# Moving the query tokens' reciprocal norms through DRAM instead of two selection matmuls, in a gated linear-attention block

## What is computed

```
q, k, v = conv4(silu(x @ Wq)), conv4(silu(x @ Wk)), conv4(silu(x @ Wv));  z = x @ Wz;  a = x @ Wa;  b = x @ Wb
q, k = rope(q), rope(k)
q = q / max(norm(q), 1e-12);  k = k / max(norm(k), 1e-12)        # per token and head
for s in range(4):                                                # four lags
    attn = sum_d(q[t] * k[t - s]) / sqrt(128)
    out[t] += attn * sigmoid(a[t - s] * b[t]) * v[t - s]
out = out * rms(out) * norm_w * silu(z);   result = out @ Wout
```

## Time and profile before

| | us |
|---|---|
| median of 3 runs | 1431.97 |
| the profiled execution's own time | 1433.0 |
| span of its trace | 1431.2 |
| PE busy in the span | 1398.2 (98%) |
| DVE, ACT, POOL busy | 1027.4, 733.4, 404.0 |
| steps of the attention stage | from about 48 to about 1005, 14.55 a step in the middle |

### The profile page before, as it was taken

One profiled execution on the slowest core, in us unless ns is written; L12 is line 12 of the kernel. 1 busy time (PEld: TensorE's weight loads), 2 busy tenths in 40 slices (PEclk: granted clock), 3 DMA queues, 4 the chain that ended last, 5 costly groups with the idle time before them and its releaser, 6 DMA issues. The chain is left out here.

```text
span 1431.2 us, 23209 instructions
## 1 busy us (share of the span) xinstructions
PE 1398.2 (98%) x7048; PEld 1166.4 (82%) x7048; DVE 1027.4 (72%) x1597; ACT 733.4 (51%) x2146; POOL 404.0 (28%) x504
## 2 busy tenths in 40 slices
PE   6999999999999999999999999997999999999998
PEld 4778888888888888888888888886788888788886
DVE  7889999999999999999989999995122222234442
ACT  5655655556655556565565665553554444332221
POOL 6152443434434344434443443422000000000001
PEclk9999999999999999999999999998899999999999
DMA  9123334433344233433334333333331101065454
GB/s 298 38 73 83 95 75 103 96 80 94 74 103 95 73 95 73 110 88 81 88 82 109 88 79 90 80 75 82 128 115 52 44 22 44 22 184 166 144 166 157
DMA packets 103962, 137.60 MB, mean 96 GB/s; under 512 B 11248, under 2 KB 48112, under 8 KB 103664
## 3 DMA queue, kind: packets, MB, share of 16 engines
q1 hardware_dynamic: 94704, 120.28, 29.4%
q0 software_dynamic: 9216, 16.78, 6.7%
HBM read 61.53 MB, written 25.17 MB: 61 GB/s over the span
## 5 line engine op out<-in xcount | busy, mean ns | idle before, releaser
L428 POOL TENSOR_TENSOR rnorm<-norms,neg_half 128x8 f32<-128x8 f32 x64 | 126.8, 1982 | 353.1 <-DVE norms L660 353.1
L635 DVE SCALAR_TENSOR_TENSOR y_k<-u_k,cw_k,y_k 128x512 f32<-128x512 f32 x192 | 159.6, 831 | 26.4 <-ACT y_k L533 18.1
L635 DVE SCALAR_TENSOR_TENSOR y_v<-u_v,cw_v,y_v 128x512 f32<-128x512 f32 x192 | 172.7, 899 | 6.9
L553 ACT ACTIVATE bank<-bank 128x128 f32<-128x128 f32 x512 | 133.6, 261 | 85.7 <-PE bank L826 85.7
L1137 DVE TENSOR_TENSOR hid_lo<-relu,hid_hi 128x512 fp32r<-128x512 f32 x64 | 44.3, 692 | 179.0 <-ACT hid_hi L1083 179.0
L635 DVE SCALAR_TENSOR_TENSOR y_q<-u_q,cw_q,y_q 128x512 f32<-128x512 f32 x192 | 144.4, 752 | 31.6 <-ACT y_q L533 23.5
L1055 POOL TENSOR_TENSOR g_buf<-g_buf,up_raw 128x512 f32<-128x512 f32 x3 | 3.8, 1282 | 411.0 <-DVE g_buf L1158 411.0
L1178 DVE TENSOR_TENSOR hid_lo<-o_raw,hid_hi 128x512 fp32r<-128x512 f32 x64 | 44.3, 692 | 102.9 <-ACT hid_hi L1103 102.9
L1079 ACT ACTIVATE relu<-bank,us_sb 128x512 f32<-128x512 f32 x64 | 44.0, 688 | 127.9 <-PE bank L1218 127.9
L1103 ACT ACTIVATE hid_hi<-o_raw 128x512 fp32r<-128x512 f32 x64 | 40.4, 632 | 123.5 <-PE bank L1248 120.8
L1233 PE MATMUL bank<-down_sign,hid_hi 128*128 128x512 f32 x256 | 101.4, 396 | 0.3 <-DVE hid_lo L1137 0.3
(11 more groups left out here) (173 smaller groups left out, 3565.5 us busy)
## 6 DMA issues: line engine op xcount, KB each, us to landing
swapped_q<-y_q SPq DMA_DIRECT2D x128, 128.0 KB, 2.3
swapped_k<-y_k SPq DMA_DIRECT2D x128, 128.0 KB, 2.3
sq_sum<-out_sq POOLq DMA_DIRECT2D x64, 256.0 KB, 3.4
o_scratch<-o_buf SPq DMA_DIRECT2D x64, 256.0 KB, 2.5
o_raw<-o_scratch SPq DMA_DIRECT2D x64, 256.0 KB, 3.2
raw_q<-in_wq SPq DMA_DIRECT2D x16, 256.0 KB, 3.1
raw_k<-in_wk SPq DMA_DIRECT2D x16, 256.0 KB, 3.6
raw_v<-in_wv SPq DMA_DIRECT2D x16, 256.0 KB, 4.5
```

The costliest lines, as they stand in the source:

```text
L428: nc.gpsimd.tensor_tensor(rnorm[:, g1 % 2, :], norms[:, g1 % 2, :], neg_half[:, 0:2 * BC], ALU.pow).then_inc(root_done, 1)
L553: last = nc.scalar.activation(block_of, block_of, ACT.Square, accum_out=norms[:, g1 % 2, i * BC + b:i * BC + b + 1])
L635: nc.vector.scalar_tensor_tensor(y[n][:, g % 2, :], u[n][:, g % 2, i:i + CH], cw[n][:, bass.ds(h * TAPS + i, 1)], y[n][:, g % 2, :], ALU.m ...
```

## The change

The reciprocal norms of the query tokens take another way. Once POOL has them (`root_done`), SP stores those of the group to a small DRAM scratch, `rq_scratch[g]`, as rows of 4 numbers (the four blocks of the group) per token, 128 rows, with four more rows behind them that hold the first four tokens of the following block. That is three DMAs: the group's own 128 x 4, the 4 x 3 of the blocks within it, and the 4 x 1 that the group before lacked (zeros behind the last group). A step later in the pipeline one load brings each partition 8 rows (128 B): the 4 from the multiple of four at or below its token, and the next 4. Those rows overlap, four partitions read the same ones. POOL masks the 8 rows with a constant table (`window`: from the own token on in the first four, before it in the second), adds the two halves, and multiplies by gate_k. The result is `gates`, which DVE uses as before. Gone are rq_x, rq_parts, sel_r, both matmuls, the copy that made sel_r, and DVE's join and product. The floor of the norms moves from DVE to POOL, and POOL's wait for gate_done to its first gate_k.

```
 # SP, step(h, g), ahead of the swaps
+                if at := back(h, g, 1):
+                    g1 = at[1]
+                    wait(sp, root_done, c)
+                    own = rnorm[:, g1 % 2, 0:BC]
+                    sp.dma_start(rq_scratch[g1, 0:P, :], own).then_inc(rq_stored, 16)
+                    sp.dma_start(rq_scratch[g1, P:P + LAGS, 0:BC - 1], own[0:LAGS, 1:BC]).then_inc(rq_stored, 16)
+                    first = own[0:LAGS, 0:1] if g1 > 0 else rot["q"][0:LAGS, S:S + 1]
+                    sp.dma_start(rq_scratch[(g1 - 1) % G, P:P + LAGS, BC - 1:BC], first,
+                                 allow_slow_non_contiguous=True).then_inc(rq_stored, 16)
 # SP, behind the swaps, ahead of the output's store
+                if at := back(h, g, 2):
+                    g2 = at[1]
+                    wait(sp, rq_stored, 48 * (c if back(h, g, 1) else c - 1))
+                    runs = bass.AP(tensor=rq_scratch.tensor, offset=rq_scratch[g2].offset,
+                                   ap=[[LAGS * BC, P // LAGS], [0, LAGS], [1, WIN * BC]])
+                    sp.dma_start(rq_win[:, g2 % 2, :, :].rearrange("p j b -> p (j b)"), runs).then_inc(rq_in, 16)
 # POOL, step(h, g)
                 if at := back(h, g, 1):
+                    wait(pool, norms_done, c)
+                    pool.sem_inc(norms_seen, 1)
+                    nc.gpsimd.tensor_scalar(norms[:, g1 % 2, :], norms[:, g1 % 2, :], NORM_FLOOR, None, ALU.max
+                                            ).then_inc(floor_done, 1)
                     wait(pool, floor_done, c)
+                    wait(pool, rq_stored, 48 * (c - 2))
                     nc.gpsimd.tensor_tensor(rnorm[:, g1 % 2, :], norms[:, g1 % 2, :],
                                             neg_half[:, 0:2 * BC], ALU.pow).then_inc(root_done, 1)
                     wait(pool, root_done, c)
-                    nc.gpsimd.tensor_tensor(rq_x[:, :, :], *spread, ALU.mult).then_inc(rq_spread, 1)
-                    nc.gpsimd.tensor_tensor(rq_parts[:, blocks, 0, :], *spread, ALU.mult).then_inc(rq_spread, 1)
-                    nc.gpsimd.tensor_tensor(rq_parts[:, blocks, 1, :], ..., ALU.subtract).then_inc(rq_done, 1)
+                    if is_start(h, g - 1):
+                        pool.wait_ge(gate_done, 2)
                     nc.gpsimd.tensor_tensor(gate_k[:, g1, :, :], ...)
+                if at := back(h, g, 2):
+                    g2 = at[1]
+                    win = rq_win[:, g2 % 2, :, :]
+                    wait(pool, rq_in, 16 * (c - 1))
+                    nc.gpsimd.tensor_tensor(win, win, window[:, :, None].broadcast_to([P, WIN, BC]), ALU.mult
+                                            ).then_inc(rq_masked, 1)
+                    wait(pool, rq_masked, c - 1)
+                    nc.gpsimd.tensor_tensor(rq_own[:, :, :], win[:, 0:LAGS, :], win[:, LAGS:WIN, :], ALU.add
+                                            ).then_inc(rq_joined, 1)
+                    wait(pool, rq_joined, c - 1)
+                    wait(pool, rnorm_done, c - 1)
+                    wait(pool, gated, c - 2)
+                    nc.gpsimd.tensor_tensor(gates[:, :, :], rq_own[:, :, :].rearrange("p r b -> p b r"),
+                                            gate_k[:, g2, :, :], ALU.mult).then_inc(gates_done, 1)
                 if g == 1 and back(h, g, 0) and not (isinstance(h, int) and h == 0):
                     split_lo("z", h)
                 if g == 3 and not is_last(h):
                     for n in "qkv":
                         split_lo(n, h + 1)
 # DVE, step(h, g): at the start, and ahead of the gating
-                    wait(dve, norms_done, c)
-                    nc.vector.tensor_scalar(norms[:, g1 % 2, :], norms[:, g1 % 2, :], NORM_FLOOR, None, ALU.max
-                                            ).then_inc(floor_done, 1)
-                    wait(dve, rq_picked, c - 1)
-                    nc.vector.tensor_reduce(gates[:, :, :], ...).then_inc(rq_joined, 1)
-                    nc.vector.tensor_tensor(gates[:, :, :], gates[:, :, :], gate_k[:, g2, :, :], ALU.mult
-                                            ).then_inc(gates_done, 1)
 # PE, step(h, g), ahead of the scores
-                    wait(pe, rq_done, c - 1 + ahead)
-                    wait(pe, gates_done, c - 2)
-                    nc.tensor.matmul(bank_rq[:, 0:2 * BC * LAGS], sel_r[:, 0, :], own, start=True, stop=False)
-                    nc.tensor.matmul(bank_rq[:, 0:2 * BC * LAGS], sel_r[:, 1, :], after, start=False, stop=True
-                                     ).then_inc(rq_picked, 1)
```

More of the change, by code:

```diff
@@ L122, in gated_recurrent_block_kernel @@
         period = const[:, C_PER:C_PER + LAGS]
+        window = const[:, C_WIN:C_WIN + WIN]
         banks = [top.enter_context(nc.psum_tensor(f"bank{i}", [P, 512], fp32)) for i in range(4)]
@@ L153, in attention @@
     (fp32, f32r, ALU, ACT, P, S, HID, KT, H, D, CH, G, BC, NB, LAGS, HALO, TAPS, BW, AB, SCALE, LN_EPS,
-     NORM_FLOOR, sb, sem, wait) = (
+     NORM_FLOOR, WIN, sb, sem, wait) = (
         env[n] for n in ("fp32", "f32r", "ALU", "ACT", "P", "S", "HID", "KT", "H", "D", "CH", "G", "BC", "NB",
[L156 to L160, removed]
+                         "LAGS", "HALO", "TAPS", "BW", "AB", "SCALE", "LN_EPS", "NORM_FLOOR", "WIN", "sb",
+                         "sem", "wait"))
+    (const, neg_half, x_hi, x_lo, sq_sum, ident, sel_own, sel_next, band, period, window, banks, pair, banks2, cw,
+     gate0, raw, w_hi, w_lo, raw_in, whi_done, wlo_done, w_slice, nw_sb, us_sb, o_scratch, up_raw, down_raw, ones,
+     ones_set, o_stored, rq_scratch) = (
         env[n] for n in ("const", "neg_half", "x_hi", "x_lo", "sq_sum", "ident", "sel_own", "sel_next", "band",
-                         "period", "banks", "pair", "banks2", "cw", "gate0", "raw", "w_hi", "w_lo", "raw_in",
+                         "period", "window", "banks", "pair", "banks2", "cw", "gate0", "raw", "w_hi", "w_lo", "raw_in",
                          "whi_done", "wlo_done", "w_slice", "nw_sb", "us_sb", "o_scratch", "up_raw",
-                         "down_raw", "ones", "ones_set", "o_stored"))
+                         "down_raw", "ones", "ones_set", "o_stored", "rq_scratch"))
     sum_squares, SQ_EARLY = env["sum_squares"], env["SQ_EARLY"]
@@ L176, in attention @@
         rnorm = sb("rnorm", [P, 2, 2 * BC], at=ctx)
-        rq_x = sb("rq_x", [P, BC, LAGS], at=ctx)
-        rq_parts = sb("rq_parts", [P, (NB + 1), 2, LAGS], f32r, at=ctx)
-        sel_r = sb("sel_r", [P, 2, P], f32r, at=ctx)
+        rq_win = sb("rq_win", [P, 2, WIN, BC], at=ctx)
+        rq_own = sb("rq_own", [P, LAGS, BC], at=ctx)
         gate_k = sb("gate_k", [P, G, BC, LAGS], at=ctx)
@@ L261, in attention @@
         rnorm_done = sem("rnorm_done", ctx)
-        rq_spread = sem("rq_spread", ctx)
-        rq_done = sem("rq_done", ctx)
-        rq_picked = sem("rq_picked", ctx)
+        norms_seen = sem("norms_seen", ctx)
+        rq_stored = sem("rq_stored", ctx)
+        rq_in = sem("rq_in", ctx)
+        rq_masked = sem("rq_masked", ctx)
         rq_joined = sem("rq_joined", ctx)
-        sel_done = sem("sel_done", ctx)
         scores_done = sem("scores_done", ctx)
@@ L366, in _ @@
                 env["load_ffn_weights"](sp, i)
+            sp.wait_ge(cleared, 5)
             schedule(sp, step)
@@ L418, in _ @@
             pool.wait_ge(const_in, 16)
-            pool.wait_ge(gate_done, 2)
-            pool.wait_ge(cleared, 6)
+            pool.wait_ge(cleared, 5)
             def step(h, g):
@@ L788, in _ @@
             project_ab(3)
-            pe.wait_ge(cleared, 6)
+            pe.wait_ge(cleared, 5)
             def turn_v(g1, c):
@@ L1296, in shape_constants @@
         (p[:, None] % lags) == np.arange(lags)[None, :],
+        np.arange(lags)[None, :] >= (p[:, None] % lags),
+        np.arange(lags)[None, :] < (p[:, None] % lags),
     ], axis=1).astype(np.float32)
```

27 lines of the change are left out of this document (5 added, 22 removed).

## The result

The changed kernel takes 1460.71 us (median of 4 runs, 1453.88 to 1467.62) against 1431.83 of the kernel before: a ratio of 1.0202, 95% interval 1.0172 to 1.0231. The forecast was 1454, slower, with a range of 1436 to 1482. The profiled execution took 1456.69, its span is 1454.9, 23.7 more than that of the kernel before.

A forecast was written before the change was run, and what follows sets the result against it. PE bounded the kernel, busy 200.00 of 200 us in the middle windows. Pair -9.0, stops +31.5, start -4.6 and end +4 made +21.9 us on 1433.0, an execution 1.0 above the median, hence 1454 us; range 1436 to 1482.

The forecast's parts named there:

- The order on POOL (part 3): At a head's last step, next head's wlo_q split waits behind the window on POOL; 15 stops of 2.1 us, 31.5 more.
- a rival at 0.14: Each 2.1 us stop at a head's end also costs the clock, 24 us more, 1478 us in all; chance 0.14.
- The pair (part 1): Two selection matmuls gone from PE's stream: 0.14 us a pair, 64 pairs, 9.0 us less.
- DVE, and the ordinary steps (parts 2, 4): Work moved off DVE and within POOL costs nothing; ordinary steps hide the window with 0.7 us to spare.
- The start (part 5): At the third step, PE's wait for rq_parts and the low clock behind it vanish: 4.6 us less.
- The end (part 6): In the last steps, stores and load put the first accumulating DMA 3.9 us later; 4 us more (2 to 6).
- The sum: Whole kernel: the terms give +21.9 us on the profiled execution's 1433.0, which stands 1.0 above the median; forecast 1454 us.

The follow-up runs named there:

- the first experiment: Changed kernel with the three splits of q, k and v ahead of the window wait on POOL in a head's last step; 1415.85 us, ratio 0.9885.
- the sixth experiment: Kernel before with only POOL's wait for gate_done moved to its first gate_k, both matmuls kept; 1427.1 us, ratio 0.9969.
- the fifth: Kernel before without its two selection matmuls and without any trip through DRAM (its output differs); 1413.4 us, ratio 0.9862.
- the third experiment: Changed kernel with POOL's product with gate_k moved behind the split of q in a head's last step; 1441.54 us, ratio 1.0068.
- the second: Changed kernel with the window's load issued on SP between the swaps of q and those of k; 1417.31 us, ratio 0.9894.
- the last experiment: Changed kernel with both the splits ahead of the window on POOL and the load ahead of k's swaps on SP; 1418.09 us, ratio 0.9897.
- The fourth experiment: Changed kernel with the split of k ahead of that of q in a head's last step; 1493.45 us, ratio 1.0424.

## Why the prediction was right, point by point

**The order on POOL (part 3).** Right in mechanism, place, count and nearly in size: 15 stops of 2.1 were forecast, 31.5 us, and 34.7 came. (Without rounding up at each link, the forecast's own terms give 627.1 and 2.0 a stop, 30 us; and its lower bound of 1.0 a stop should have been 625.9 - 625.1 = 0.8.) The links, in the step shown above: the taps of k at 2.33 (right, and for the reason given: with the split beside them again, in the first experiment, they take 3.22); the load out 1.23 instead of 1.10 us behind the swaps' start; landed in 2.0/2.0/3.8 us (min, median, max) instead of 2.3; POOL's three operations 1.86 to 2.02 in the longer stops and 1.47 in the shorter ones (574.36 to 575.83) instead of 1.4; the split 1.70 instead of 1.63; PE 0.06 behind it instead of 0.2, a term for which the prediction had no row. The landing of 2.0 is what the Trainium skill's formula gave (DMA: Bandwidth & Descriptors, "Anatomy of one DMA": 2.04 for 16 KB); on this point the page was nearer than the rows that I took, which were of larger transfers. (The page's fit is of the GpSimd path and this load goes out on SP's queue, so this is one agreement and not a test of the formula.)

**The clock.** This is the largest term that the sum left out, 7.6 us in the profiled execution. I put it to a rival at 0.14 as all or nothing: 15 falls at 1.6 us each, or none. The price was right (1.5 to 1.6 each) and the alternative wrong. In the profiled execution five of the eight stops of 2.5 us and more were followed by a fall, and none of the seven of about 1.95; by the mean granted clocks two of the other executions had more falls and one had fewer. With five falls, the forecast would have been 1454 + 5 x 1.6 = 1462. The prediction also says that the trace before shows a restart at half rate once, at the start; it has another at the end of the attention stage, where the granted clock is 0.50 from 995 to 1010 us.

**The pair (part 1).** 9.0 forecast; 0.21 x 64 = 13.5 measured (12.8 over the 60 steps counted above). The term was mis-sized because its price was read at the start of the scores and not at the next group behind them.

**DVE, and the ordinary steps (parts 2, 4).** Right: PE waits in none of them, and DVE's slack is worth nothing by itself. DVE's idle time before q's taps, waiting for ACT, rose from 23.5 to 103.7 us.

**The start (part 5).** Right: 4.6 forecast, 4.7 measured; the moved wait alone gives 4.5 in the sixth experiment, and the fifth, without the pair and PE's waits for it but with POOL's wait in its old place, gives 4.7.

**The end (part 6).** 4 forecast, 1.0 to 1.4 measured. I gave the stores 2.2 us to land, but SP, which waits for them, sent the load 1.15 us after it began to issue the last one; and the load was in after 2.1 instead of 2.3. The shift of 3.9 at the first accumulating DMA was 1.4.

**The sum.** The errors of +3.2 (stops), +7.6 (clock), -3.8 (pair, over the 60 steps), -0.1 (start), -3.0 (end) and the -2.1 before the first step add to +1.8 us, which is 23.7 in the span against a forecast of 21.9. So errors of 10.8 one way and 9.0 the other nearly cancelled, and that the number came so close on the profiled execution is in part luck; the order on POOL, the term that decides the sign, is not. The profiled execution's 1456.69 is 4 us below the median of four, and the distance from there to 1460.71 is only in part accounted for, by the clock.

## What to carry to other kernels

When work is moved to a queue that runs in order, the first question is what already stands behind the new wait, not how long the new work is: here POOL sat idle for 7.7 us, waiting for the window, while a split of 1.7 us that it could have done in that time, as the first experiment shows, stood behind that wait and PE needed it next; moving three lines turned 2% slower into 1.1% faster. Price a small matmul in a dense stream by the distance between the groups on either side of it, with it and without it, and past the group that follows. And when a bottleneck engine is made to stop, add the clock's price to the stop's, and allow for it happening at only a part of the stops.

## What the runs showed of the hardware

**In PE's dense stream the longer stops cost the clock, and length alone doesn't decide it.** In the profiled executions the clock never fell at 23 stops of 1.3 to 2.0 us (15 in the third experiment, 7 in the changed kernel, 1 in the second); at eight of 2.5 to 3.2 it fell five times; at 15 of 3.6 to 4.3 it fell 14 times. A fall cost 1.35 to 1.6 us, two longer ones 2.4 and 2.8. Six of the stops in the changed kernel were of the same 2.31 us idle: the clock fell at three of them and not at the other three. The windows behind one of each, the stops that ended at 275.73 and at 457.68:

```profile
275.00:279.00 4.00, 3.27 (x8) 2.59 (x9) 2.47 (x3) 0.88 (x7) 4.00 (x4) 0.62 0.30 104
```

```profile
457.00:461.00 4.00, 3.32 (x14) 2.73 (x15) 2.44 (x3) 0.96 (x7) 4.00 (x4) 1.00 0.30 103
```

Nor is a short stop free of it everywhere. At the end of the attention stage, where PE has little and small work, the clock of the last experiment's kernel fell behind a stop of 1.84 us idle:

```profile
969.38 2.10 PE L901 MATMUL bank<-rot_q,rot_k 128*128 128x132 f32 x8 [1.84 <-DVE coef L733]
```

```profile
969.00:973.00 4.00, 3.62 (x17) 3.65 (x18) 1.51 (x3) 0.00 (x0) 0.64 (x1) 0.57 0.59 135
```

The Trainium skill (TensorE: Matmul & The Clock Gate, "HAM oscillation") describes the case in which every wait on a DMA is followed by a restart at half rate. The fourth experiment is nearly that case, with POOL's split in the DMA's place (14 of 15), and the third, in its profiled execution, has none of it (0 of 15).

**The same POOL operation takes 0.24 or 0.79 us, by some tens of ns of DVE's timing.** POOL and DVE of the changed kernel at a shorter stop, against the longer one above:

```profile
574.36 0.24 POOL L462 TENSOR_TENSOR rq_win<-rq_win,const 128x32 f32<-128x32 f32 x1 [7.67 <-DMA rq_win<-rq_scratch]
```

```profile
574.39 0.76 DVE L672 TENSOR_TENSOR swapped_q<-swapped_q,sin 128x512 f32<-128x512 f32 x1
```

Here POOL's mask begins 0.03 us ahead of DVE's product and takes 0.24; at 634.35 it begins 0.01 behind it and takes 0.79, until DVE's product is over. It is so at all 15 stops: in the seven shorter ones the mask begins 0.02 to 0.08 us ahead of the product and takes 0.24 to 0.26, in the eight longer ones it begins between 0.02 ahead and 0.15 behind and takes 0.64 to 0.81. That is most of the 0.58 us between the two usual lengths of stop, and only the longer ones were followed by a fall of the clock, five of the eight. The Trainium skill says of these engines (GPSIMD Engine Reference, "Specifications") that they share their way into SBUF and that DVE instructions with two SBUF inputs contend for it; DVE's product is one, and the rows agree. That the one excludes the other was not tested by itself.

What stays open is which of the stops of about 2.5 us cost the clock; no run here separates that.
